# Register loads of several words in one instruction, and a softmax ahead of the edge list's wait

## The chip, the cores and the metric
The kernel runs on one core of a Trainium2 chip. Its time is that of the device for one execution, in microseconds (us); less is better. The core's engines are TensorE (PE, its weight loads PEld), VectorE (DVE), ScalarE (ACT), GpSimd (POOL) and SyncE (SP). [...] An engine's sequencer also runs small instructions of its own, such as a load of a register from memory; in the profile those stand under the engine's name with a q behind it (DVEq, PEldq).

## What is computed
A graph network on 6250 nodes with 128 features and 100000 edges sorted by their target, in four blocks. Each block ends in a layer norm of its input plus its result.

```python
x = layernorm(x + attention_by_edge_type(x))   # block 0
x = layernorm(x + three_gat_layers(x))         # block 1: 3 layers of graph attention
x = layernorm(x + edge_mlp(x, edge_attr))      # block 2
x = layernorm(x + degree_scaled_sum(x))        # block 3
# block 0
pk    = softmax(confounder_probs)              # 5 values
alpha = einsum('ehk,k->eh', leaky_relu(scores), pk)
a     = exp(alpha - segment_max(alpha)[seg]);  alpha_n = a / segment_sum(a)[seg]
out   = segment_sum(xj * alpha_n * importance[type], dst) + x @ W[0] + bias
# a layer of block 1
e     = leaky_relu(alpha_s[src] + alpha_d[dst])
alpha = exp(e - segment_max(e)[dst]) / (segment_sum(...)[dst] + 1e-16)
out   = segment_sum(xs[src] * alpha, dst) + bias
# block 2
h = relu(concat(x[src], edge_attr) @ w1a + b1a); h = relu(h @ w1b + b1b); h = h @ w1c + b1c
agg = segment_sum(h, dst) / max(count, 1);  z = relu(concat(x, agg) @ w2a + b2a) @ w2b + b2b
# block 3
agg = segment_sum((deg**-0.5 * x)[dst], src);  out = relu(deg**-0.5 * agg @ weight.T)
```

## The kernel before
The start counts degrees with matmuls of one-hot rows (`STEPS` turns of two halves: DVE compares at L490 and L492, PE counts at L733), orders the nodes by degree and lays out records: with each group of edges, which rows of a node table to gather, and the number of the tile of target nodes that the sum is added to. In its first microseconds SP issues the DMA of the edge list and 14 weight DMAs in a row; POOL lays constants and then fills a large tile with zeros (L433); DVE splits the edge list into high and low parts (L469 to L473), waits for all weights and makes the softmax of the five mixture probabilities (L476 to L484), with ACT's exponential (L800) in its middle; PE multiplies the weights with the attention vectors (L742 to L746) and then counts.

Every later block is a loop in which POOL issues indirect DMAs. Each fetches 128 rows of a table by their numbers, or in the last block adds 128 rows to a table. The order of the work is written out by hand: each engine has its own loop over items, and semaphores free buffers.

- Layer 0 (gathers L986): items of three groups, two buffers. ACT lays out the slots (`lay_slots`, L1009, whose places in `win` it loads at L1012), makes exponentials, and keeps the running sums in `acc` at a tile number (`keep`, loads at L1047 and L1048).
- Graph attention (`gat`, L1588; gathers L1716, 16 per batch, 50 batches a layer). DVE makes the scores (`scores`), then for each half of the heads (`f` = 0, 1) the products of weights and gathered rows (L1859 to L1863) and a running sum along the slots (the scan L1872). After the second half's products it frees the batch's gather buffer (`used`), after the scans it copies the last column of each group to its tile in `acc1` (L1881). It needs two tile numbers (L1877) and two columns (L1875), each read into a register with a `value_load`. While it does so, ACT copies and writes the hidden edge features of the next block (L1797), which PE multiplies (L1727).
- Edge MLP (gathers L2012 and L2017, five per item, 224 items). DVE adds the two gathered parts (`join`, L2087), PE transposes (L2038) and multiplies (L2048), ACT applies the first ReLU (L2069), DVE adds the second ReLU to `total` at the item's tile (L2109), whose number it reads at L2104. SP fetches these numbers four items at a time (`fetch_tiles`) when DVE has freed the buffer (`tiles_free`, L2114).
- Scatter (L2449, four per item, 200 items). PE makes the messages of an item with a matrix of `same` target and `h` at four tile numbers (L2257), which it reads at L2254; ACT copies them out of PSUM (L2319), POOL adds them to memory.

A `value_load` is three sequencer instructions: the load of one word (TENSOR_LOAD), arithmetic on it (FUSED_REGOPS) and a check of its bounds (SEQ_ASSERT).

## Time and profile before
| what | us |
|---|---|
| median of 3 runs | 9856.31 (9853.96 to 9918.93) |
| the profiled execution: its own time | 9892.94 |
| its span | 9891.2 |
| TensorE, busy | 4460.2 (45%) |
| VectorE, busy | 5073.3 (51%) |
| ScalarE, busy | 1673.0 (17%) |
| GpSimd, busy | 5779.6 (58%) |

The mean granted clock of TensorE was 0.666 of its full speed. Busy time counts the engines' own operations; the sequencers' loads and waits are not in it. The start takes the first 443 us, layer 0 goes to 2110, the graph attention layers to 3550, 4920 and 6282, the edge MLP from 6375 to 8215, the scatter from 8270 to 9780; between them stand short stages without gathers. In the rows below "[5.40 <-DMA soft]" behind an operation is the time its engine sat idle before it and what released it; "issue" is idle time in which nothing that the profile shows was waited for, and "remote" a semaphore whose sender the profile doesn't name.

### The profile page before, as it was taken

The page shows a single profiled execution, that of the slowest core. Times are in us where ns is not written, and L with a number is a line of the kernel's source. Part 1 is how long each engine was busy: PE and PEld are TensorE (multiplying, and loading weights), DVE is VectorE, ACT ScalarE, POOL GpSimd, SP SyncE. Part 2 cuts the span into 40 slices and gives each one's busy share as a digit, 9 for nine tenths or more (in the row PEclk, how much of TensorE's full clock was granted, in tenths as well). Part 3 has the DMA queues.
Part 4 walks back from the last instruction along what each step waited for, and adds up shares of the span by engine and source line. Part 5 has one row for each costly group of instructions (what it writes and reads, how often), then busy time and mean ns, then how long its engine had stood idle before and what let it go on. Part 6 is the DMA issues. An engine that isn't in the chain of part 4 may idle for free. (4 is left out here: it accounts for less than half of the span.)

```text
span 9891.2 us, 83332 instructions
## 1 busy us (share of the span) xinstructions
PE 4460.2 (45%) x14438; PEld 2760.1 (28%) x14438; DVE 5073.3 (51%) x11750; ACT 1673.0 (17%) x3458; POOL 5779.6 (58%) x5435
## 2 busy tenths in 40 slices
PE   6266676762333332222232222366666666554442
PEld 5122232232222222212121121233333333343332
DVE  7266676674555544544544444444444444554443
ACT  1322222231111111111111111211111111110002
POOL 2455555525655545555555555455556555888886
PEclk8688888875555565555565555677778777765555
DMA  2422222234332323333233333344444444444444
GB/s 59 134 51 51 52 53 54 53 40 132 90 87 79 85 69 83 87 83 89 78 89 84 88 84 83 97 127 126 133 131 134 127 125 51 36 36 36 36 36 85
DMA packets 673823, 804.66 MB, mean 81 GB/s; under 512 B 312241, under 2 KB 513273, under 8 KB 672600
## 3 DMA queue, kind: packets, MB, share of 16 engines
q0 software_dynamic: 317520, 531.92, 26.6%
q1 hardware_dynamic: 313896, 114.11, 4.5%
q10 hardware_dynamic: 42336, 157.90, 4.5%
q14 instruction: 51, 0.42, 0.0%
q8 instruction: 20, 0.33, 0.0%
HBM read 578.06 MB, written 225.40 MB: 81 GB/s over the span
## 5 line engine op out<-in xcount | busy, mean ns | idle before, releaser
L1716 POOL DMA_INDIRECT big<-table_layer,slot_rows_L x2400 | 2298.3, 958 | 1726.5 <-issue 1138.5
L2449 POOL DMA_INDIRECT sums_by_source<-big,to x800 | 1261.3, 1577 | 282.2 <-issue 202.8
L986 POOL DMA_INDIRECT big<-table_layer,idx_L x912 | 931.7, 1022 | 767.0 <-DVE h L1160 442.1
L1735 PE MATMUL own_ps_L<-of_tile_L,big 50*128 50x16 f32 x1224 | 283.1, 369 | 2327.1 <-DVE fade_L L1850 1406.0
L2017 POOL DMA_INDIRECT big<-table_layer,rec_m x904 | 866.8, 959 | 275.4 <-issue 270.5
L2109 DVE SCALAR_TENSOR_TENSOR big<-ps,nbb,big 128x128 f32 x1792 | 545.8, 346 | 923.6 <-remote 592.6
L2048 PE MATMUL ps<-big,w 128*128 128x512 f32 x1792 | 914.3, 658 | 135.5 <-ACT big L2069 103.8
L1735 PEld LDWEIGHTS own_ps_L<-of_tile_L,big 50*128 50x128 f32 x1224 | 271.3, 324 | 2406.0 <-issue 2397.6
L1727 PE MATMUL psH_L<-w,h 128*128 128x256 f32 x1584 | 676.3, 606 | 462.2 <-ACT big L1797 385.1
L1078 PE MATMUL sums_L<-h,ident 128*128 128x512 f32 x1344 | 706.1, 674 | 322.1 <-issue 165.4
L1872 DVE TENSOR_TENSOR_SCAN big<-h,products_L 128x1122 f32<-128x1122 f32 x300 | 747.5, 2492 | 25.4 <-issue 1.0
L2257 PE MATMUL psM<-h,big 128*128 x1600 | 383.9, 415 | 618.5 <-issue 618.5
L1727 PEld LDWEIGHTS psH_L<-w,h 128*128 128x128 f32 x1584 | 484.9, 317 | 589.4 <-issue 282.1
L1797 ACT ACTIVATE big<-psH_L 128x1536 f32<-128x1536 f32 (+1 forms) x144 | 193.6, 1344 | 2657.8 <-DMA h<-in_edges 1545.0
L1863 DVE TENSOR_TENSOR products_L<-products_L,big 128x512 f32<-128x512 f32 x600 | 612.2, 1066 | 0.0
L1859 DVE COPY products_L<-big 128x66 f32<-128x66 f32 x300 | 82.5, 275 | 929.9 <-ACT products_L L1785 524.2
L2038 PE MATMUL psX<-ident,big 128*128 128x128 f32 x1800 | 299.5, 321 | 558.9 <-DVE big L2087 500.8
L2069 ACT ACTIVATE big<-psX,ba 128x512 f32<-128x512 f32 x450 | 283.5, 684 | 1573.2 <-remote 991.7
L2012 POOL DMA_INDIRECT big<-hidden_edge_parts,rec_m x226 | 213.0, 942 | 543.5 <-DVE big L2087 426.6
L2257 PEld LDWEIGHTS psM<-h,big 128*128 128x128 f32 x1600 | 330.6, 305 | 684.3 <-issue 684.3
L2048 PEld LDWEIGHTS ps<-big,w 128*128 128x128 f32 x1792 | 369.3, 218 | 529.1 <-issue 430.4
L1078 PEld LDWEIGHTS sums_L<-h,ident 128*128 128x128 f32 x1344 | 281.8, 217 | 754.2 <-issue 737.4
(445 smaller groups left out, 7361.0 us busy)
## 6 DMA issues: line engine op xcount, KB each, us to landing
hidden_edge_parts<-big ACTq DMA_DIRECT2D x72, 768.0 KB
hidden_edge_parts<-big ACTq DMA_DIRECT2D x72, 640.0 KB
big<-table_layer,slot_rows_L POOLq DMA_INDIRECT x2400
h<-in_edges ACTq DMA_DIRECT2D x75, 384.0 KB
h<-in_edges ACTq DMA_DIRECT2D x75, 320.0 KB
table_layer<-xr SPq DMA_DIRECT2D x49, 298.0 KB
big<-table_layer,idx_L POOLq DMA_INDIRECT x912
big<-table_layer,rec_m POOLq DMA_INDIRECT x904
```

Of the source, the lines that this page charges most:

```text
L986: G.indirect_dma_start(out=g[b][:, u, s, :], out_offset=None, in_=table, in_offset=bass.IndirectOffsetOnAxis(ap=at, axis=0)).then_inc(gath ...
L1078: PE.matmul(sums[b][u][:, 0:T * D], ident[:, :], prod[PROD[u]][:, s, :], start=(s == 0), stop=False, skip_group_check=True)
L1716: G.indirect_dma_start(out=ring[b][:, s, :], out_offset=None, in_=tab1_d[l], in_offset=bass.IndirectOffsetOnAxis(ap=at_rows[b][:, s, R_POS ...
L1727: last = PE.matmul(psH[:, c * HID:(c + 1) * HID], eT[b % 2][:, c * P:(c + 1) * P], w1[:, 1, :], start=True, stop=True)
L1735: last = PE.matmul(own_ps[:, c * SLOTS:(c + 1) * SLOTS], own1T[:, c * P:(c + 1) * P], of_tile[b % 2][:, :], start=True, stop=True)
L1863: last = V.tensor_tensor(p4[:, c, 0:C, 1:SLOTS + 1], bc(wt[:, hd, :], 1, C), ring[b][:, :, hd * C:(hd + 1) * C].rearrange("p s c -> p c s" ...
L1872: V.tensor_tensor_scan(flat(tot[b % 2][:, rows, :]), flat(shrink[:, rows, :]), flat(prod[:, :, :]), 0.0, ALU.mult, ALU.add)
L2017: G.indirect_dma_start(out=gx[u][:, s, :], out_offset=None, in_=tab2_d, in_offset=bass.IndirectOffsetOnAxis(ap=rec[q][:, a, s * FW + R_POS ...
L2048: last = PE.matmul(ps2[u % 2][:, f * S * P:(f + 1) * S * P], w2[:, k, f * P:(f + 1) * P], h1[u % 2][:, k * S * P:(k + 1) * S * P], start=( ...
L2109: V.scalar_tensor_tensor(t, ps2[u % 2][:, (f * S + s) * P:(f * S + s + 1) * P], nbb[:, f:f + 1], t, ALU.max, ALU.add)
L2257: last = PE.matmul(psM[v][:, s * P:(s + 1) * P], same[v][:, s, :], flat(h[:, ds(js[s], 1), :]), start=True, stop=True)
L2449: G.indirect_dma_start(out=sum_d[s], out_offset=bass.IndirectOffsetOnAxis(ap=to[u][:, s:s + 1], axis=0), in_=msg[u][:, s, :], in_offset=No ...
```

## The change
Two things. First, in all gather loops one `load` reads several neighbouring words of a tile into several registers, and a `snap` for each register gives the value with its bounds; before, each value had a `value_load`. In the graph attention the tile numbers are copied beside the columns into one tile of four words (`places`), with one more cast in `scores`, and all four are read in the second half, behind its scan. In the edge MLP the four tile numbers of four items are read at the first of them, and the buffer is freed right behind that load. Second, the probabilities are SP's first DMA, with a semaphore of their own, and DVE makes their softmax before it waits for the edge list; the other waits for weights count 13 instead of 14 DMAs.

```diff
--- before.py
+++ after.py
@@ -276,6 +276,7 @@
             edges_in = sem("edges_in_d")
             cst2 = sem("consts_first")
             w_in = sem("weights_in")
+            probs_in = sem("probs_in")
             x_in = sem("features_in")
             wp = sem("score_weights_done")
             w_ok = sem("score_weights_copied")
@@ -329,14 +330,14 @@
 
             @block.sync
             def _(sp):
+                sp.dma_start(soft[:, :], probs.partition_broadcast(P)).then_inc(probs_in, 16)
                 sp.dma_start(e32[:, :], dst).then_inc(edges_in, 16)
                 for to, frm in ((wT[:, :, :], W0T), (aI[:, :], attI), (aJ[:, :], attJ),
                                 (rhs0[:, :, 0:D], W0), (bias[:, 0, :], bias0.partition_broadcast(P)),
                                 (wsT[:, :, :], WsT), (wdT[:, :, :], WdT),
                                 (aS[:, :, :], attS), (aD[:, :, :], attD), (rhs1[:, :, 0:D], Ws),
                                 (impt[:, :], importance.partition_broadcast(P)),
-                                (bias[:, 1:4, :], bias1.partition_broadcast(P)), (bias1T[:, :], bias1cols),
-                                (soft[:, :], probs.partition_broadcast(P))):
+                                (bias[:, 1:4, :], bias1.partition_broadcast(P)), (bias1T[:, :], bias1cols)):
                     sp.dma_start(to, frm).then_inc(w_in, 16)
                 sp.dma_start(xTs[:, :], xT).then_inc(x_in, 16)
                 sp.sem_inc(rec_out, 64)
@@ -432,7 +433,7 @@
 
                 G.memset(pool1[:, :], 0.0).then_inc(blank, 1)
                 pool.wait_ge(cst2, NCONST)
-                pool.wait_ge(w_in, 16 * 14)
+                pool.wait_ge(w_in, 16 * 13)
                 G.tensor_tensor(out=rhsN[:, 0:D], in0=rhs0[:, 0, 0:D], in1=ident[:, :], op=ALU.add)
                 pool.wait_ge(w_ok, 1)
                 pool.wait_ge(soft_ok, 1)
@@ -465,6 +466,16 @@
                 for v in range(STG):
                     last = V.memset(stage[v][:, :, A0:A0P], 0.0)
                 last.then_inc(pos_blank, 1)
+                dve.wait_ge(probs_in, 16)
+                V.tensor_reduce(tot[:, 0:1], soft[:, :], AX.X, ALU.max)
+                dve.drain()
+                V.tensor_scalar(soft[:, :], soft[:, :], tot[:, 0:1], None, ALU.subtract).then_inc(mx, 1)
+                dve.wait_ge(ex, 1)
+                V.tensor_reduce(tot[:, 1:2], soft[:, :], AX.X, ALU.add)
+                dve.drain()
+                V.reciprocal(tot[:, 2:3], tot[:, 1:2])
+                dve.drain()
+                V.tensor_scalar(soft[:, :], soft[:, :], tot[:, 2:3], None, ALU.mult).then_inc(soft_ok, 1)
                 dve.wait_ge(edges_in, 16)
                 V.tensor_scalar(part[0][:, :], e32[:, :], P - 1, None, ALU.bitwise_and)
                 V.tensor_scalar(part[1][:, :], e32[:, :], 7, None, ALU.arith_shift_right)
@@ -472,16 +483,6 @@
                 V.tensor_copy(lo[:, :], part[0][:, :])
                 V.tensor_copy(hi[:, :], part[1][:, :])
                 dve.drain()
-                dve.wait_ge(w_in, 16 * 14)
-                V.tensor_reduce(tot[:, 0:1], soft[:, :], AX.X, ALU.max)
-                dve.drain()
-                V.tensor_scalar(soft[:, :], soft[:, :], tot[:, 0:1], None, ALU.subtract).then_inc(mx, 1)
-                dve.wait_ge(ex, 1)
-                V.tensor_reduce(tot[:, 1:2], soft[:, :], AX.X, ALU.add)
-                dve.drain()
-                V.reciprocal(tot[:, 2:3], tot[:, 1:2])
-                dve.drain()
-                V.tensor_scalar(soft[:, :], soft[:, :], tot[:, 2:3], None, ALU.mult).then_inc(soft_ok, 1)
                 dve.wait_ge(cst2, NCONST)
                 with dve.Fori(0, STEPS) as i:
                     for v in range(2):
@@ -737,7 +738,7 @@
                     pe.sem_inc(c, 1)
                 pe.wait_ge(cst2, NCONST)
                 PE.matmul(histp[:, 0:NT], zerob[:, :], zerob[:, 0:NT], start=True, stop=False)
-                pe.wait_ge(w_in, 16 * 14)
+                pe.wait_ge(w_in, 16 * 13)
                 for t in range(T4):
                     PE.matmul(wps[:, t * 40:t * 40 + 20], wT[:, t, :], aJ[:, :], start=True, stop=True)
                     PE.matmul(wps[:, t * 40 + 20:t * 40 + 40], wT[:, t, :], aI[:, :], start=True, stop=True)
@@ -1009,7 +1010,8 @@
                     def lay_slots(b, i):
                         act.wait_ge(slots_out[b], i * 32 + 32)
                         act.sem_inc(gate_a, 1)
-                        at = [0] + [act.value_load(spot[b][0:1, u:u + 1], min_val=0, max_val=SLOTS - S) for u in range(1, B)]
+                        act.load(spot_r, spot[b][0:1, 1:B])
+                        at = [0] + [act.snap(r, min_val=0, max_val=SLOTS - S) for r in spot_r]
                         A.activation(flat(win[b][:, :, :]).bitcast(u16), flat(padw[:, :, :]).bitcast(u16), ACT.Copy)
                         A.drain()
                         for u in range(B):
@@ -1031,6 +1033,8 @@
                     act.sem_inc(tiles_read, 2)
                     act.sem_inc(shr_ok, 1)
                     n = turns(act)
+                    tile_r = [act.alloc_register(f"tile_{tag}_r{u}") for u in range(B - 1)]
+                    spot_r = [act.alloc_register(f"spot_{tag}_r{u}") for u in range(1, B)]
                     exps(0, 0, 0)
                     shrinks(0, 0)
                     lay_slots(0, 0)
@@ -1045,7 +1049,8 @@
                         for b in range(2):
                             k = i * 2 + b
                             js = [act.value_load(tile[1 - b][0:1, B - 1:B], min_val=0, max_val=NT)]
-                            js += [act.value_load(tile[b][0:1, u:u + 1], min_val=0, max_val=NT) for u in range(B - 1)]
+                            act.load(tile_r, tile[b][0:1, 0:B - 1])
+                            js += [act.snap(r, min_val=0, max_val=NT) for r in tile_r]
                             A.drain().then_inc(tiles_read, 1)
 
                             act.wait_ge(z_ok, k + 1)
@@ -1597,7 +1602,7 @@
                     of_tile = [sb(f"of_tile_{tag}{v}", [NTP, SLOTS], fp32, ph) for v in range(2)]
                     same = sb(f"same_tile_{tag}", [1, GPB, GS], fp32, ph)
                     in_tile = sb(f"slots_in_tile_{tag}", [1, GPB], fp32, ph)
-                    last_col = sb(f"last_column_{tag}", [1, GPB], i32, ph)
+                    places = sb(f"tile_and_column_{tag}", [1, 2 * GPB], i32, ph)
                     z = sb(f"z_{tag}", [P, H, SLOTS], fp32, ph)
                     zc = sb(f"zc_{tag}", [P, H, SLOTS + 1], fp32, ph)
                     lift = sb(f"lift_{tag}", [P, H, SLOTS + 1], fp32, ph)
@@ -1838,7 +1843,8 @@
                             V.tensor_reduce(in_tile[:, :], same[:, :, :], AX.X, ALU.add)
                             V.scalar_tensor_tensor(z[:, :, :], z[:, :, :], 0.2, z[:, :, :], ALU.mult, ALU.max)
                             dve.drain()
-                            V.tensor_copy(last_col[:, :], in_tile[:, :])
+                            V.tensor_copy(places[:, GPB:2 * GPB], in_tile[:, :])
+                            V.tensor_copy(places[:, 0:GPB], tiles[:, :, 0])
                             V.tensor_scalar(zc[:, :, 1:SLOTS + 1], z[:, :, :], LOW, None, ALU.max)
                             dve.drain()
                             V.tensor_tensor_scan(flat(run_max[:, :, :]), flat(lift[:, :, :]), flat(zc[:, :, :]), 0.0,
@@ -1872,10 +1878,9 @@
                                 V.tensor_tensor_scan(flat(tot[b % 2][:, rows, :]), flat(shrink[:, rows, :]), flat(prod[:, :, :]),
                                                      0.0, ALU.mult, ALU.add)
                                 if f:
-                                    ks = [dve.value_load(last_col[0:1, u:u + 1], min_val=1, max_val=GS) for u in range(GPB)]
-                                else:
-                                    js = [dve.value_load(fl[b][0:1, GS * u, R_J:R_J + 1], min_val=0, max_val=NT)
-                                          for u in range(GPB)]
+                                    dve.load(places_r, places[0:1, :])
+                                    js = [dve.snap(r, min_val=0, max_val=NT) for r in places_r[0:GPB]]
+                                    ks = [dve.snap(r, min_val=1, max_val=GS) for r in places_r[GPB:]]
                                 dve.drain()
                             for u in range(GPB):
                                 V.tensor_copy(flat(acc1[:, ds(js[u], 1), :]),
@@ -1933,6 +1938,7 @@
                             V.tensor_tensor(brow[:, :], brow[:, :], psB[0:4, :], ALU.add).then_inc(rows_read, 1)
                         dve.drain()
                         n = turns_of_batches(dve)
+                        places_r = [dve.alloc_register(f"tile_or_column_{tag}{u}") for u in range(2 * GPB)]
                         one_hot(0, 0)
                         both_loops(dve, n, turn)
                         if counting:
@@ -2092,6 +2098,7 @@
                     dve.sem_inc(summed, 2)
                     dve.sem_inc(joined, U)
                     n = turns(dve)
+                    tile_r = [dve.alloc_register(f"tile_m_r{a}") for a in range(Q)]
                     join(0, 0)
                     join(0, 1)
                     with dve.Fori(0, n) as i:
@@ -2100,8 +2107,11 @@
                             join(*following(*following(i, u)))
                             if u % Q == 0:
                                 dve.wait_ge(tiles_in[q], i * 16 + 16)
-                            dve.sem_inc(gate_v, 1)
-                            j = dve.value_load(tiles[q][:, u % Q, R_J:R_J + 1], min_val=0, max_val=NT)
+                                dve.sem_inc(gate_v, 1)
+                                dve.load(tile_r, tiles[q][:, :, R_J])
+                                js = [dve.snap(r, min_val=0, max_val=NT) for r in tile_r]
+                                dve.sem_inc(tiles_free[q], 1)
+                            j = js[u % Q]
                             dve.wait_ge(lin2, g + 3)
                             for s in range(S):
                                 for f in range(2):
@@ -2110,8 +2120,6 @@
                                                            ALU.max, ALU.add)
                                 last = V.drain()
                             last.then_inc(summed, 1)
-                            if u % Q == Q - 1:
-                                dve.sem_inc(tiles_free[q], 1)
 
             fresh_semaphores()
             added = [sem(f"added_{s}") for s in range(S)]
@@ -2251,7 +2259,8 @@
                         pe.wait_ge(same_ok, g + 1)
                         pe.wait_ge(msg_ok, g + 1)
                         pe.sem_inc(gate_pe, 1)
-                        js = [pe.value_load(rec[u][0:1, s, R_J:R_J + 1], min_val=0, max_val=NT) for s in range(S)]
+                        pe.load(tile_r, rec[u][0:1, :, R_J])
+                        js = [pe.snap(r, min_val=0, max_val=NT) for r in tile_r]
                         pe.sem_inc(tiles_read, 1)
                         for s in range(S):
                             last = PE.matmul(psM[v][:, s * P:(s + 1) * P], same[v][:, s, :], flat(h[:, ds(js[s], 1), :]),
@@ -2271,6 +2280,7 @@
                             if early and u == 5:
                                 output(q, n)
 
+                    tile_r = [pe.alloc_register(f"tile_s_r{s}") for s in range(S)]
                     pe.sem_inc(msg_ps, 2)
                     pe.sem_inc(tiles_read, U)
                     for w in range(2):
```

## Rows read from the trace of the kernel before

**Rows 1.** Windows by stage: us, busy us (count) of PE, PEld, DVE, ACT, POOL; clock, DMA, GB/s.
```profile
443.00:2110.00 1667.00, 1129.08 (x2212) 457.21 (x2213) 1116.77 (x2460) 362.17 (x1053) 931.70 (x912) 0.83 0.31 52
...
3620.00:4920.00 1300.00, 319.44 (x931) 253.03 (x930) 608.97 (x1236) 168.04 (x146) 755.61 (x800) 0.55 0.31 85
...
6375.00:8215.00 1840.00, 1153.90 (x3559) 603.48 (x3560) 852.85 (x2655) 280.44 (x446) 1079.79 (x1130) 0.79 0.47 130
8270.00:9780.00 1510.00, 682.06 (x2788) 539.40 (x2788) 675.16 (x1778) 171.54 (x332) 1261.29 (x800) 0.59 0.41 36
```
**Rows 2.** Waits in the scatter, 8350 to 9700: us in total, times, longest.
```profile
POOL sums_by_source L2449 <- issue: 181.1, 594, 0.3
```
**Rows 3.** Waits in the edge MLP, 6500 to 8050.
```profile
DVE big L2109 <- remote: 488.3, 62, 12.0
...
POOL big L2012 <- DVE big L2087: 361.9, 65, 9.2
```
**Rows 4.** Timeline in the edge MLP: start us, us, operation, count [idle before <-releaser].
```profile
7206.21 3.60 PE L2048 MATMUL ps<-big,w 128*128 128x512 f32 x8
...
7212.85 0.95 POOL L2017 DMA_INDIRECT big<-table_layer,rec_m  x1 [0.30 <-issue]
7215.30 2.66 DVE L2109 SCALAR_TENSOR_TENSOR big<-ps,nbb,big 128x128 f32 x8 [10.07 <-remote]
...
7218.08 1.43 DVE L2087 TENSOR_TENSOR big<-big 128x256 f32<-128x256 f32 x4
...
7220.34 0.94 POOL L2012 DMA_INDIRECT big<-hidden_edge_parts,rec_m  x1 [6.54 <-DVE big L2087]
```
**Rows 5.** Timeline of the start, DVE.
```profile
3.90 2.06 DVE L469 TENSOR_SCALAR pool<-pool 128x784 int32<-128x784 int32 x1 [2.84 <-DMA pool<-in_dst]
...
7.15 0.64 DVE L473 CAST hi_d<-pool 128x784 bf16<-128x784 int32 x1
...
13.42 13.40 DVE L478 TENSOR_SCALAR soft<-soft,tot 128x5 f32<-128x5 f32 x1
...
27.93 1.09 DVE L490 TENSOR_TENSOR oneL<-lo_d,wide 128x1792 bf16<-128x1792 bf16 x1
```
**Rows 6.** Timeline of the start, POOL.
```profile
10.50 15.87 POOL L433 MEMSET pool<- 128x18944 f32 x1
```
**Rows 7.** Lines, 0 to 443: count, busy us, mean ns, idle before and releasers.
```profile
L490 DVE TENSOR_TENSOR oneL<-lo_d,wide 128x1792 bf16<-128x1792 bf16 x56 | 61.2, 1093 | 7.9 <-PE histp L733 7.8
```
**Rows 8.** Timeline of the start, PE.
```profile
18.77 0.57 PE L746 MATMUL wps<-aD,wdT 128*128 128x4 f32 x2
29.54 0.67 PE L733 MATMUL histp<-oneH,oneL 128*128 128x49 bf16 x5 [10.19 <-DVE oneH L492]
```
**Rows 9.** Instructions of line 1877: count, ns min/median/max, first and last start.
```profile
L1877 DVEq TENSOR_LOAD <-slot_records_L x300: 7/302/1029, 2265.2 to 6291.9; - x150
L1877 DVEq FUSED_REGOPS  x300: 190/190/728, 2266.1 to 6292.2; - x150
```
**Rows 10.** Timeline in the second graph attention layer.
```profile
4218.65 2.49 DVE L1872 TENSOR_TENSOR_SCAN big<-h,products_L 128x1122 f32<-128x1122 f32 x1
...
4221.21 0.27 DVE L1859 COPY products_L<-big 128x66 f32<-128x66 f32 x1
...
4224.27 0.94 POOL L1716 DMA_INDIRECT big<-table_layer,slot_rows_L  x1 [16.77 <-issue]
```
**Rows 11.** Waits in the second graph attention layer, 3800 to 4600.
```profile
DVE big L1881 <- issue: 72.6, 62, 7.1
```
**Rows 12.** Instructions of line 1012 in layer 0.
```profile
L1012 ACTq TENSOR_LOAD <-spot_L x171: 272/277/283, 470.1 to 2125.2; - x171
```
**Rows 13.** Waits in layer 0, 600 to 2100.
```profile
ACT big L1024 <- DVE carry_L L1173: 119.0, 38, 7.1
```
**Rows 14.** Instructions of line 2254 in the scatter.
```profile
L2254 PEldq TENSOR_LOAD <-rec_s x800: 293/298/397, 8267.9 to 9718.0; - x160
```

## What I predict

> **What bounds the kernel now.** I read the busy times by stage first, then what GpSimd's gathers wait for in each stage, then single stretches in order of time. The page's average (POOL 58% busy) says little, since the stages differ [rows 1]. In the last stage, the scatter, POOL is busy 1261.29 of 1510 us in 800 DMA issues of 1.58 us, and its idle time there is "issue" of 0.3 us between two of them [rows 1, 2]: it never waits for another engine's result, so whatever TensorE's loads cost there is off the path. In the gather stages POOL issues in bursts and then stands: 1667 - 931.70 = 735 us idle in layer 0, 1300 - 755.61 = 544 us in a graph-attention layer, 1840 - 1079.79 = 760 us in the edge MLP [rows 1]. Part of it is the 0.3 us behind each of 800 to 1130 gathers. The rest are true pauses: in the edge MLP POOL waited 361.9 us for the join of DVE, and DVE's sums waited 488.3 us for "remote" [rows 3].
>
> One pause in order of time shows the chain [rows 4]. TensorE began its matmuls at 7206.21, but DVE's sums of their result start at 7215.30, 1.5 us after POOL's last gather of the burst (7212.85 + 0.95). The sums take 2.66 us, the join behind them 1.43, and POOL restarts at 7220.34. No register load is exposed in that chain: sums end at 7217.96, the join starts at 7218.08. So this pause is one of completions that come late, not of address arithmetic. The question for every load that the change drops is whether it lies in such a chain or under another instruction.
>
> **The softmax ahead of the edge list.** Now DVE splits the edge list (3.90 on), waits for the last of the weight DMAs, and then its subtraction of 128x5 stands from 13.42 for 13.40 us, to 26.82; the one-hot loop starts at 27.93 [rows 5]. POOL has been filling a 128x18944 tile from 10.50 to 26.37 [rows 6], so the subtraction stood behind the fill. TensorE had finished its weight products at 19.34 (18.77 + 0.57) and counts from 29.54 [rows 8].
> After the change the probabilities are the first DMA and should land by about the 3.90 at which the first one now does. The bitwise operation issued at 3.90 ended at 5.96 [rows 5], beside POOL's first constant, so I let the subtraction end there too; from the subtraction's end to the loop the exponential, sum, reciprocal and product took 27.93 - 26.82 = 1.1 us [rows 5]: softmax done at 7.1. The four edge operations take 4 x 0.64 = 2.6 us [rows 5] and end at 9.7. The fill starts at 10.50. The loop can start at about 10.6, 17 us earlier; but TensorE is in order behind its weight products, whose DMAs are unchanged but for one, so it counts from 19.34 instead of 29.54: **-10.2 us**. The loop itself is DVE's (56 x 1.09 us for the larger half alone, and 7.8 us waiting for TensorE) [rows 7], and the ordering, scores and table follow its end, so I count the shift in full.
> It hangs on the loop's first comparison running beside the fill. No row shows a two-input DVE operation beside a POOL fill; the only operation beside it, the subtraction, was held to its end. By the pessimist's end the comparison starts at 26.4 and the shift is 29.54 - 28.2 = **-1.3**; the optimist's end, were TensorE not in order, is -17. I take -10, as the comparison is another kind of operation.
> [...]
>
> **Graph attention, three layers.** Each of 150 batches reads two tile numbers after DVE's first scan and two columns after the second; the change reads all four after the second, and casts two more values. One value costs a load of 0.30 us and 0.19 for its register arithmetic [rows 9], with check and gaps about 0.6; two are 1.2 us, issued when the scan starts. The scan takes 2.49 us (4218.65 to 4221.14) and the next operation starts at 4221.21 [rows 10]: both pairs lie wholly under a scan. Four words in one load are 0.30 + 4 x 0.28 = 1.4 us, also under it. The cast adds some 0.2 us per batch, 30 us in all of DVE, but the stage waits on POOL. So nothing in most batches.
> There are stretches in which a sequencer instruction takes 0.7 us (maxima 1029 for the load, 728 for the arithmetic) [rows 9]; the accumulating copies behind them sat idle up to 7.1 us, 72.6 us in 62 times [rows 11]. There two values cost 6 x 0.7 = 4.2 us, 1.7 us beyond the scan. The first pair is ahead of the products that free the ring for POOL, so its removal takes 1.7 us off; the second block grows to 9 x 0.7 = 6.3 us, 3.8 beyond its scan, but POOL had restarted by then (4224.27, during the second scan [rows 10]). An estimate: a quarter of 100 batches in two layers x 1.7 = 43 us of DVE, of which a quarter is in the chain that POOL waits for (72.6 us of such idle against 544 of pauses says no more): **-10 us**, between -75 (each slow batch counts, both blocks) and +15 (the cast in half the batches).
>
> **Edge MLP.** DVE read one tile number per item; now it reads four at every fourth, 56 times. One took 0.30 us [rows 9] and was issued under the 1.43 us join [rows 4]: hidden, so the three dropped gain nothing. Four words are issued just behind the join's four operations and end 1.4 us later, an estimated 0.3 us after it; in about half the items DVE waits on a late completion anyway [rows 3]. 56 x 0.3 x 1/2 = **+8 us**, between 0 and +59 (56 x 1.05, each further word 0.2 us more). Freeing the tile buffer before the sums instead of after the fourth lets SP fetch sooner, four items ahead: nothing waits for that DMA now.
> [...] No multi-word load is in this trace; the single one took 0.30. [...]
>
> **Layer 0.** ACT reads three slots in one load instead of three, 57 times, and three tiles in one (0.28 us for a load [rows 12]): at most 2 x 57 x 2 x 0.28 = 64 us of ACT's sequencer. Those are ahead of a wait for DVE's carry (119.0 us in 38 waits [rows 13]), so what ACT gains it waits. POOL's pauses here end with DVE's own work, which no changed instruction feeds directly: **-3**, between -20 and 0.
>
> **Scatter.** TensorE drops 3 of 4 loads per item, 200 x 3 x 0.30 = 180 us [rows 14] of its own idle time. POOL's 7.5 us per item covers it [rows 1, 2]: **0**.
>
> **The sum.** -10 -10 -3 +8 = -15 us. Against the profiled run's own 9892.94 that is 9878; that run lies 36.6 us above the median, so on the median 9856.31 it gives **9841**.
>
> **Rivals.**
> A. *The fill blocks the comparison, or the edge operations are late.* If the last cast is issued after 10.50, or the comparison collides, the start gives 1.3 instead of 10. For: the held subtraction, and only 0.8 us of room. Against: another kind of operation. 9850. Chance 0.25.
> B. *Bursts join (faster).* A pause costs about 7 us (7213.80 to 7220.34 [rows 4]). If DVE's shorter sequencer work lets a batch's buffer come free before POOL runs dry, whole pauses vanish: 5 in each attention layer are 105 us, 9841 - 105 = 9736. For: pauses, not gathers, are what can shrink; slow stretches hold DVE up. Against: the chain behind a pause shows no load. 0.14.
> C. *Bursts split (slower).* In the attention layers DVE's block after the second scan is longer. POOL restarts during that scan and has two buffers of 16 gathers, 2 x 20 us; if the block delays the next freed buffer by over about 5 us, each such batch costs a pause of 7 us; with the edge MLP's +59 in place of +8, and four pauses in each layer, 9841 + 51 + 84 = 9976. It decides at 5 us; by my count the slow block is 2.1 us longer than before (3.8 - 1.7). 0.06.
> D. *One instruction is not one cost:* the load is split or pays by word, so the loads give nothing and only the start remains: 9846 to 9871. 0.15.
>
> **The numbers.** 1% is what a measurement of this kernel can tell, 98.6 us: 9757.7 and 9954.9. The forecast itself has 0.40; with A and D that is 0.80 within 1%, from about 9790 to 9890. B gives 0.14 faster, C 0.06 slower. For 8 in 10 the range leaves out most of B and of C: the low end is -75 in the attention layers (9841 - 65 = 9776), the high end the +59 of the edge MLP, or D, or a few split bursts (9841 + 51 = 9892): 9775 to 9890.
>
> **What would show it.** The subtraction at about 4 to 6 us; the first comparison at 10.6 (or 26.4: A); TensorE's first count at about 19.4. In the attention layers the scan followed by the next copy within 0.1 us, as now, and idle before the accumulating copies no longer than before. In the edge MLP an "issue" idle of 0.2 to 0.4 us at every fourth item (1 us: D). In the scatter less idle of TensorE and the same stage time. Wrong would be: a stage of gathers that moves by over 40 us either way while its POOL busy time stays, since then pauses, not loads, changed.

## The result and the profile after

The changed kernel took 9786.39 us (median of 4 runs, 9761.33 to 9800.99), the kernel before 9870.99 in the runs beside it: ratio 0.990 (95% interval 0.9866 to 0.9934), 85 us less. The profiled execution took 9785.20 us, 107.7 less than that of before. I had forecast 15 us.

First the windows by stage, as in [rows 1] (us, busy us and count of PE, PEld, DVE, ACT, POOL; clock, DMA share, GB/s), each cut around the stage's gathers:

```profile
431.00:2067.00 1636.00, 1124.60 (x2213) 456.42 (x2214) 1115.11 (x2459) 361.40 (x1055) 944.16 (x912) 0.83 0.31 54
2190.00:3514.00 1324.00, 408.15 (x1745) 327.02 (x1745) 706.64 (x1379) 198.65 (x170) 785.17 (x801) 0.55 0.34 93
3588.00:4855.00 1267.00, 315.71 (x928) 251.80 (x928) 613.28 (x1279) 168.04 (x146) 756.98 (x800) 0.56 0.32 87
4912.00:6180.00 1268.00, 322.62 (x946) 254.48 (x946) 622.07 (x1290) 168.04 (x146) 759.90 (x800) 0.56 0.32 88
6272.00:8109.00 1837.00, 1169.50 (x3560) 596.33 (x3560) 855.94 (x2656) 279.24 (x444) 1082.30 (x1130) 0.79 0.47 130
8165.00:9671.00 1506.00, 693.05 (x2776) 541.08 (x2776) 669.23 (x1774) 171.00 (x331) 1261.20 (x800) 0.57 0.41 36
```

POOL's busy time in the second attention layer is what it was (756.98 against 755.61), so the stage is shorter by pauses alone. From the first to the last gather the stages changed so: layer 0 -31 us, attention layers +8, -32 and -33, edge MLP 0, scatter 0; the first gather starts 12 us earlier. The idle times of POOL over 1 us, called its pauses from here on, went from 32 to 24 and from 32 to 25 in attention layers 2 and 3.

The start, DVE, then POOL's fill, then PE (against [rows 5, 6, 8]):

```profile
4.14 1.43 DVE L472 TENSOR_SCALAR soft<-soft,tot 128x5 f32<-128x5 f32 x1
...
8.18 0.66 DVE L484 CAST hi_d<-pool 128x784 bf16<-128x784 int32 x1
10.47 1.09 DVE L491 TENSOR_TENSOR oneL<-lo_d,wide 128x1792 bf16<-128x1792 bf16 x1 [1.64 <-POOL rgrid L431]
...
19.22 1.09 DVE L491 TENSOR_TENSOR oneL<-lo_d,wide 128x1792 bf16<-128x1792 bf16 x1 [5.80 <-PE histp L734]
```
```profile
10.07 15.91 POOL L434 MEMSET pool<- 128x18944 f32 x1
```
```profile
17.15 0.57 PE L747 MATMUL wps<-aD,wdT 128*128 128x4 f32 x2
17.58 2.79 PE L734 MATMUL histp<-oneH,oneL 128*128 128x49 bf16 x28
```

The subtraction takes 1.43 us instead of 13.40, and the comparison runs its usual 1.09 us inside the fill. TensorE counts from 17.58 instead of 29.54; DVE waits 5.80 us for its first count.

In the kernel before each `value_load` of L1877 left three records on DVE's sequencer, 300 TENSOR_LOADs and 300 FUSED_REGOPS [rows 9] and as many checks (count, ns min/median/max):

```profile
L1877 DVEq SEQ_ASSERT  x300: 5/23/730, 2266.4 to 6292.4; - x150
```

The loads after, in the order graph attention, layer 0, edge MLP, scatter:

```profile
L1881 DVEq TENSOR_LOAD <-tile_and_column_L x150: 338/351/1228, 2228.1 to 6192.2; - x150
L1013 ACTq TENSOR_LOAD <-spot_L x57: 694/701/712, 458.8 to 2081.7; - x57
L2111 DVEq TENSOR_LOAD <-tiles_m x56: 947/954/976, 6293.2 to 8100.9; - x56
L2262 PEldq TENSOR_LOAD <-rec_s x200: 987/994/1107, 8160.1 to 9606.4; - x100
```

On DVE four neighbouring words took 0.35 us, on DVE and TensorE four that lie a record apart 0.95 and 0.99, on ACT three neighbours 0.70. No FUSED_REGOPS or SEQ_ASSERT stands at those lines any more: the words are used as loaded, one FUSED_REGOPS follows at the next line (medians of 0.08 us at L1014, 0.10 at L2263, 0.12 at L1882 and L2112), and the page counts 78407 instructions instead of 83332.

And the idle time of DVE before its accumulating copies in the second attention layer (3750 to 4850), before and then after:

```profile
DVE big L1881 <- issue: 109.5, 82, 7.1
```
```profile
DVE big L1886 <- issue: 18.0, 88, 0.2
```

That is the second thing to see: 1.3 us per copy became 0.2, and the longest idle fell from 7.1 us to 0.2. The slow stretches are not gone, though. Among the operations of `scores` the same kind of idle is as long as before or longer (one operation of them in the same window, before and then after):

```profile
DVE run_max_L L1844 <- issue: 20.2, 20, 1.2
```
```profile
DVE run_max_L L1850 <- issue: 48.8, 14, 3.9
```

Counted from first to last gather of attention layers 2 and 3, DVE's "issue" idle in `scores` was 210 and 217 us and is 222 and 209; where nothing pauses (after_c, below) it is 1 us at most. SyncE still has 139 and 143 small instructions of 0.7 us (148 and 163 before; 685 to 735 ns, drains left out). What is gone is DVE's long idle behind its two scans.

### The profile page after: what moved, and what is told of

It reads as the page before. It is cut to its first block and busy times, and to the rows that moved or that the text cites. A ratio compares the mean times of both kernels' runs of the same rounds, so it can differ in the third digit from the quotient of the medians.

```text
span 9783.2 us, 78407 instructions
## 1 busy us (share of the span) xinstructions
PE 4485.3 (46%) x14438; PEld 2759.3 (28%) x14438; DVE 5075.9 (52%) x11900; ACT 1671.1 (17%) x3458; POOL 5792.4 (59%) x5435
```

## The experiments

Theory S: where POOL gathers in long bursts, sequencer instructions of DVE, ACT and SP are at times served one per 0.70 us; the change helps because DVE and ACT issue far fewer register instructions (DVE 2 a batch in place of 12). Rival M: it helps because one read stands in place of several. Rival P: it helps because no load stands ahead of the products that free the ring.

**The setting.** One fact cuts through all runs. On four chips (numbers 3, 11, 15 and 2) the kernel before took 8208 to 8210 us, on four others (8, 7, 1 and 0) 9824 to 9906, like the first measurement. The program is the same and POOL's busy time nearly so; POOL's pauses over 1 us add up to 37, 34, 15, 15 and 0 us in the five gather stages (soft_only, chip 3) instead of 466, 296, 305, 305 and 435. Below, a chip "pauses" or it doesn't; there is one trace for each variant, and those of the pausing kernels come from several chips. From first to last gather, in us (the first row is the trace of before; "one-word", "padded" and "moved" are the variants described below):

| trace | pauses | first gather at | layer 0 | att. 1 | att. 2 | att. 3 | MLP | scatter |
|---|---|---|---|---|---|---|---|---|
| before | yes | 443 | 1665 | 1312 | 1295 | 1299 | 1835 | 1505 |
| after | yes | 432 | 1634 | 1321 | 1263 | 1266 | 1835 | 1505 |
| after_again | yes | 431 | 1617 | 1313 | 1270 | 1252 | 1855 | 1504 |
| l0_only_b | yes | 439 | 1618 | 1305 | 1297 | 1279 | 1825 | 1507 |
| gat_single_b (one-word) | yes | 442 | 1628 | 1325 | 1260 | 1270 | 1821 | 1505 |
| gat_padded_c (padded) | yes | 435 | 1650 | 1331 | 1288 | 1279 | 1811 | 1509 |
| gat_moved_c (moved) | yes | 444 | 1675 | 1368 | 1297 | 1296 | 1831 | 1508 |
| mlp_tail_b | yes | 433 | 1660 | 1288 | 1299 | 1272 | 1841 | 1506 |
| soft_only | no | 401 | 1257 | 1046 | 1012 | 1016 | 1425 | 1504 |
| gat_only | no | 410 | 1255 | 1048 | 1012 | 1016 | 1425 | 1507 |
| after_c | no | 399 | 1254 | 1051 | 1013 | 1016 | 1428 | 1502 |

**1. The parts alone, where nothing pauses** (chip 3). Each is the kernel before with one part of the diff shown ahead.

> The kernel before with the softmax move alone. In the trace of the changed kernel the first gather of layer 0 started 11.6 us earlier (431.5 against 443.1). Theory: the whole of that is the softmax move, since the DVE comparison runs beside POOL's fill and TensorE's first count moves from 29.54 to 17.58; ratio 0.9988 (-12 us), first gather at 431 to 432, and every later stage as long as before: layer 0 1665, attention layers 1312, 1295 and 1299, edge MLP 1835, scatter 1505 us, each within 10 us. Rival: an earlier start shifts how GpSimd's bursts fall against the other engines and so part of the 31 us of layer 0 or of the 32 and 33 us of attention layers 2 and 3 shows here too; then one of those stages is over 15 us shorter.

Ratio 0.9988 (0.9979 to 0.9998), first gather at 401 where the others have 408 to 412: the whole gain of the start, as expected.

> The kernel before with the graph attention's part alone (four words in one load behind the second scan). Theory: DVE's stretches of 0.7 us per sequencer instruction disappear with two thirds of the register instructions; the 33.2 and 31.8 us that DVE lost between first scan and next product in layers 2 and 3 come back in full, so those two layers take about 1263 and 1266 us instead of 1295 and 1299, the first layer 1312 to 1320, total -57 us, ratio 0.9942. Rival 1: the gain of those layers came from elsewhere (start, layer 0, chance of a run), and they stay within 10 us of before. Rival 2, what the prediction had: -10 us.

> The kernel before with layer 0's part alone (two loads of three words on ACT). Theory: layer 0 takes about 1634 us instead of 1665 (-31), by fewer sequencer instructions of ACT in the chain behind the exponentials; all else as before, ratio 0.9969. Rival 1: ACT's loads are ahead of a wait anyway (the prediction): within 5 us of 1665. Rival 2: the 31 us were a run's chance or came with the earlier start.

> The kernel before with the edge MLP's and the scatter's parts alone. Theory: neither is on the path of POOL; edge MLP 1835 and scatter 1505 us as before within 8 us, ratio 1.000. The four-word loads take 0.95 (DVE) and 0.99 us (TensorE) each, against 0.30 for one word. Rival: each loses its own way, the edge MLP by 56 x 0.65 = 36 us of DVE for the longer load, so a ratio of 1.004.

1.0003 (0.9993 to 1.0012), 1.0004 (0.9994 to 1.0013) and 0.9995 (0.9985 to 1.0004). Every load is hidden here, as the prediction had it, and so neither gain of theory S appears; these expectations had been made for a kernel with pauses.

**2. The whole change again** (chip 8, which pauses).

> The changed kernel once more, against the kernel before. In the runs of the four parts the kernel before took 8208 us, not 9856, and GpSimd's pauses in the gather stages were 37, 34, 15, 15 and 0 us instead of 466, 296, 305, 305 and 435; the parts other than the softmax moved nothing. Theory: where those pauses are missing, only the start is left of the change: -10 us, ratio 0.9988, with the five gather stages as long as in the kernel before within 5 us. Where they are there (before at about 9860), the ratio is 0.990 again, with layer 0 and attention layers 2 and 3 some 31, 32 and 33 us shorter. Rival: the parts work only together, and the ratio is 0.99 in either setting.

9770.59 against 9906.13 us, ratio 0.9865 (0.9816 to 0.9914): the gain is real where POOL pauses; whether it is more than in the first measurement the two intervals don't tell.

**3. What in the attention part helps.** gat_single keeps four one-word loads in their old places and takes the values as loaded:

```diff
-  ks = [dve.value_load(last_col[0:1, u:u + 1], min_val=1, max_val=GS) for u in range(GPB)]
+  for u in range(GPB):
+      dve.load(places_r[GPB + u], last_col[0:1, u:u + 1])
+  ks = [dve.snap(r, min_val=1, max_val=GS) for r in places_r[GPB:]]
...
+  (the same for js, behind the first scan)
```

gat_padded takes the changed attention part and adds dummy reads behind its scans:

```diff
+  for _ in range(1 if f else 2):
+      dve.value_load(places[0:1, 0:1], min_val=0, max_val=NT)
```

gat_moved is the kernel before with the branch of `js` put under `if f:` beside `ks`, each still a `value_load`.

Their first runs, and gat_only twice more, fell on chips without pauses:

> The graph attention's part alone once more; what matters is whether the kernel before has its pauses in this run (about 9860 to 9910 us) or not (about 8208). Theory S: DVE's sequencer instructions inside long gather bursts are served one per 0.70 us; fewer of them means that DVE no longer meets this, so attention layers 2 and 3 take about 1265 us each instead of 1295, the first one as before, ratio 0.994, and the idle between first scan and next product is 0.07 us in every batch. Rival: those layers gain only with the other parts, ratio 1.000. Without pauses: 1.000 under both.

> The four-word load as in the change, and beside it two dummy one-word reads with their checks in the first half's place and one in the second's, so that DVE's queue again has as many register instructions as before; the values used come from the one load. Theory S (the number of instructions): the 0.7 us stretches return and most of the gain goes, ratio 0.998 to 1.000, with 25 to 35 us of excess idle behind the first scan in layers 2 and 3. Rival M (one read of memory instead of four dependent ones behind the copies): the gain stays, ratio 0.994. Without pauses: 1.000.

> The kernel before with its four one-word loads at their old places, but each value taken straight from its register, so without the arithmetic and bounds check behind each load: 4 sequencer instructions a batch instead of 12, no load of several words, no extra cast. Theory S: nearly the whole gain, ratio 0.994 to 0.996, so the load of several words is not what helps. Rival M: no gain, 1.000. Without pauses: 1.000.

> The kernel before with the two tile numbers read behind the second scan, beside the columns, four one-word loads with their checks: as many instructions as before, but none ahead of the products that free the ring. Theory P (place): the 33 us per layer that lay behind the first scan are what POOL waited for, so layers 2 and 3 gain about 30 us each though the slow stretches stay behind the second scan, ratio 0.994. Theory S alone: stretches move with the instructions, the block behind the second scan grows by 30 us a layer and POOL gains part of it at most, ratio 0.996 to 1.000. Without pauses: 1.000.

> The graph attention's part alone, again in the hope of a chip on which the kernel before pauses (two of three so far had none: 8208 us; one had them: 9906 us). With pauses, theory S (fewer sequencer instructions of DVE): attention layers 2 and 3 about 30 us shorter each, no idle over 0.1 us between first scan and next product, ratio 0.994; layer 0, edge MLP and scatter as in the kernel before. Rival: the gain needs the other parts. Without pauses: 1.000.

1.0002, 1.0002, 0.9996 and 1.0002 (chip 11), 1.000 (chip 15), every interval within 0.0015 of 1. They tell nothing of the theories. Then chip 7, which pauses:

> Four one-word loads at their old places without arithmetic and checks behind them, again for a setting with pauses. With pauses, theory S (the number of sequencer instructions): attention layers 2 and 3 gain 25 to 33 us each, ratio 0.994 to 0.996, and the idle behind the first scan is gone. Rival M (the one load of four words): 1.000. Without pauses: 1.000.

Ratio 0.9978 (0.9959 to 0.9996), attention layers 2 and 3 at 1260 and 1270 us. With no load of several words, the long idle behind the scans is gone (3750 to 4850):

```profile
DVE big L1884 <- issue: 18.4, 86, 0.5
```

Six register instructions a batch are left of twelve, and DVE still has 41 and 46 small instructions of 0.7 us in layers 2 and 3 (195 and 198 before). Rival M as the only cause is out. The ratio is smaller than I expected, though the two layers came out as expected; the runs of before on this chip have a low median (9824.4).

> Layer 0's part alone, again for a setting in which the kernel before pauses. With pauses: layer 0 takes 1615 to 1635 us against 1665, the later stages as in the kernel before, ratio 0.996 (fewer instructions of ACT's sequencer inside gather bursts). Rival: 1.000, the gain of layer 0 needs the earlier start. Without pauses: 1.000.

Layer 0 took 1618 us, but the ratio is 0.9990 (0.9972 to 1.0009): a gain in the trace that the times don't make certain.

On chip 2 nothing pauses:

> The one four-word load plus three dummy one-word reads with their checks, so DVE has its old number of sequencer instructions; again for a setting with pauses. Theory S (number): the excess idle behind DVE's first scan is back (25 to 35 us in each of layers 2 and 3), these layers take 1290 to 1300 us, ratio 0.998 to 1.001. Rival M (one read in place of several is what helps): 1260 to 1270 us each, no excess idle, 0.994 to 0.997. Without pauses: 1.000.

> All four values read one by one with their checks, behind the second scan; again for a setting with pauses. Theory P (only what stands ahead of the ring-freeing products counts): no idle behind the first scan, layers 2 and 3 at 1260 to 1270 us though the stretches behind the second scan stay, ratio 0.996. Theory S with the block's length counting in full: the excess of 33 us moves behind the second scan (from 67 to about 100 us) and the layers stay at 1280 to 1300 us, ratio 0.998 to 1.001. Without pauses: 1.000.

> The changed kernel on the same chip as the two before it. With pauses: ratio 0.988 to 0.993, start 10 us, layer 0 10 to 45 us, attention layers 2 and 3 together 55 to 75 us shorter than in the kernel before. Without pauses, theory: only the start is left, ratio 0.9988; rival: the parts add up to more, under 0.997.

1.0005 (0.9996 to 1.0015), 1.0003 (0.9993 to 1.0012) and, for the whole change, **0.9986 (0.9976 to 0.9995)**: only the start is left. Then chip 1, which pauses:

> As gat_padded_b. With pauses, theory S (number of sequencer instructions): excess idle of 25 to 35 us behind DVE's first scan in each of attention layers 2 and 3, 1290 to 1300 us each. Rival M (one read in place of several): 1260 to 1270 us each and no excess idle. Without pauses: 1.000.

Ratio 1.0031 (1.0004 to 1.0057), layers 2 and 3 at 1288 and 1279. The same line, then the dummy reads' arithmetic here and in the run of the same kernel on a chip without pauses:

```profile
DVE big L1883 <- issue: 83.5, 84, 5.6
```
```profile
L1880 DVEq FUSED_REGOPS  x450: 5/197/710, 2244.7 to 6284.3; - x150
```
```profile
L1880 DVEq FUSED_REGOPS  x450: 190/197/203, 1823.3 to 5022.4; - x150
```

With nearly the old number of instructions (11) the long idle is back, although one load reads all four words: theory S. The excess behind the first scan is smaller than expected (23.6 and 10.1 us, not 25 to 35), and the two layers lie at the low end of the kernels with that idle. The attention part of the change by itself fell on chips without pauses all three times; where POOL pauses it was seen only within the whole change. The last two rows show that the 0.7 us belongs to the setting, not to the instruction: the longest of 450 is 203 ns there.

> As gat_moved_b. With pauses, theory P (only what stands ahead of the ring-freeing products counts): no idle behind the first scan, attention layers 2 and 3 at 1260 to 1270 us, ratio 0.996. Theory S with the block's length counting in full: the layers stay at 1280 to 1300 us, ratio 0.998 to 1.002. Without pauses: 1.000.

```profile
DVE big L1880 <- issue: 194.4, 84, 14.2
```

Ratio 1.0066 (1.0028 to 1.0103) on chip 0: slower than before. No idle is left behind the first scan, yet layers 2 and 3 stay at 1297 and 1296, while the idle behind the second grew from 109.5 to 194.4 us. Rival P is out: emptying one place and filling the other gives nothing. The kernel is slower, as rival C had it for a longer block behind the second scan, but not by its mechanism: POOL has no more pauses than before (30, 31 and 32 in the three layers against 31, 32 and 32), and most of the loss is in layer 1, 1368 us against 1312, where they add up to 354 us against 296.

> The edge MLP's and the scatter's parts alone, for a setting with pauses. Theory: the four-word load of 0.95 us stands behind every fourth join and delays sums and the next burst, edge MLP 1840 to 1855 us, ratio 1.001 to 1.003; the scatter 1505 us as before. Rival: hidden by the late completions, edge MLP 1810 to 1835 us, ratio 1.000. Without pauses: 1.000.

Ratio 1.0002 (0.9974 to 1.0030), edge MLP 1841 us, scatter 1506. Waits of the sums for completions (DVE L2109 and its like, 6500 to 8050) are no fewer than in [rows 3]:

```profile
DVE big L2113 <- remote: 562.6, 77, 14.2
```

The three traces with this part have 1835 to 1855 us (mean 1844), the five without it 1811 to 1835 (1825). A cost of up to 19 us fits, the times neither confirm nor exclude it.

## Why the prediction was wrong, step by step

**What bounds the kernel.** Right in that no load stood in the chain of [rows 4], and that pauses are what can shrink. But I took the pauses for the kernel's own. Where they are missing, the edge MLP of the changed kernel waits so (5280 to 6600 of after_c):

```profile
DVE big L2093 <- DMA big<-table_layer,rec_m: 384.8, 172, 5.3
...
DVE big L2119 <- PE ps L2054: 67.6, 37, 3.5
...
POOL big L2018 <- issue: 59.7, 196, 0.3
```

No wait of DVE's sums for "remote" is left (488.3 us in [rows 3]), and POOL's gathers of this stage are never kept longer than 0.3 us. The program is the same but for the change; the late completions of [rows 4] don't show here.

**The start.** Right: forecast -10, measured 12 us in the trace and 0.9988 alone (on the pausing chips the first gather comes at 431 and 432 us with the part, at 433 to 444 without it). The comparison ran beside the fill: 1.09 us inside one of 15.91. That it would, being another kind of operation than the held subtraction, was my assumption; no row of before showed it, and no run shows why the subtraction was held and the comparison not. The comparison at 25.72, beside POOL's addition at 25.95 that reads two tiles, took 1.64. TensorE's products ended at 17.72, 1.6 us sooner than in [rows 8], which is the rest of the 12 us. Rival A did not happen; the last cast was issued at 8.18, 1.9 us ahead of the fill.

**Graph attention: the step that failed.** I put -10 us: 25 slow batches of 1.7 us are 43 us of DVE, a quarter of that on the path, and the block behind the second scan counted nothing, as POOL had restarted by then. What was mis-sized is the 43 us. In the trace of before the idle between first scan and next product exceeds 0.6 us in 7 and 8 of 50 batches of layers 2 and 3, with 33.2 and 31.8 us in all: 4 to 5 us a batch. Behind the second scan and between the copies there are another 97 and 101 us more than after the change. All of DVE's "issue" idle fell from 459 and 466 us to 332 and 332, by 261 us, and the two layers by 65: a quarter. In gat_single_b the idle fell by 368 us and the layers by 64, a sixth. So in these kernels the share was about right, and the idle six times what I had. The share is no constant: in gat_moved_c the idle is 137 us more than before and the two layers are as long.

I had it too small for three reasons that the traces show. The drains and address operations around the register instructions are served at the same pace, and I had not counted them: of DVE's 367 and 380 sequencer instructions of 685 to 735 ns in layers 2 and 3 of before, 172 and 182 are drains, and 23 and 26 the address operations of L1881. At times DVE gets only one in 1.4 us, with one of SyncE between (below). And I gave the new block nine instructions, one load and an arithmetic and a check for each word, where it has two. That the block behind the second scan is not free gat_moved_c shows.

That the stretches stay, as the sum assumed, was right: DVE still meets them in `scores`, and now also just ahead of the scans (33 and 27 us of "issue" idle against 1 and 0). But in none of the 100 batches does it stand over 0.1 us behind the first scan or over 0.5 us behind the second and between the copies.

Traces without long idle behind the scans (after, after_again, gat_single_b) have 2522 to 2530 us for layers 2 and 3 together, the five with it 2567 to 2594: -53 us on average. Part of it is given back in layer 1: 1313 to 1325 us against 1288 to 1312 in the three traces with the old attention part (gat_padded_c and gat_moved_c have 1331 and 1368). No run shows a cause. Over all three layers it is 3835 to 3855 against 3859 to 3906, 35 us on average.

**Layer 0.** I put -3, on the argument that ACT's time ahead of a wait is lost anyway. Three traces with the part have 1617 to 1634 us (mean 1623), five without it 1628 to 1675 (1656). But gat_single_b, without the part, has 1628, and the times of the part alone give -10 with an interval from -28 to +9. So the -31 of the first trace lies outside my bound of -20, and how much of it the part makes stays open.

**Edge MLP and scatter.** +8 and 0 forecast; 0 to +19 and 0 measured. The load of four took 0.95 us, where one word took 0.30 (L2104 of before): (0.954 - 0.303) / 3 = 0.217 us for each further word. No row of the kernel before shows the 0.2 us for a further word behind my +59 of the range; in its place the runs showed this 0.217, on TensorE (0.994 - 0.298) / 3 = 0.232, and on ACT, for neighbours, (0.701 - 0.277) / 2 = 0.212. In the attention layers four neighbours took 0.351 on DVE, where one had taken 0.311 (L1875 of before). Rival D was so far right: in three of the four places the load took about 0.2 us longer for each further word. In after_c the "issue" idle before the sums is never over 0.3 us, as forecast.

**The rivals.** What came nearest is B, fewer and longer bursts, at 0.14; I priced it at 105 us by 15 lost pauses, and 15 were lost (8 and 7) for 70 us. The three traces without the long idle have 24 or 25 pauses in each of these layers, the other five 26 to 32. I argued against it that the pause in [rows 4] showed no load. That pause was in the edge MLP, where nothing was gained; the case had to be read in the attention layers, whose [rows 11] showed the 7.1 us.

**The sum.** By the averages above, where POOL pauses: start -8 to -12, layer 0 up to -33, layer 1 +18, layers 2 and 3 -53, MLP up to +19: about -60 of the 85 and 135 us measured. The rest lies between the stages and in the spread of a kernel that pauses (before: 9854 to 9954 us on chip 8 alone). How these share out is not settled. That 9786 lies inside my range is owed to its low end, the -75 of the attention layers, not to the -10.

What serves the sequencers once per 0.70 us, and why only some chips do it, no run shows. That it is one thing shared by DVE and SyncE is suggested by the records at 4011 us of the trace of before, where DVE and SyncE take turns: SP at 4011.56, DVE 4012.27, SP 4012.96, DVE 4013.67.

## What to carry to other kernels

Before costing a load by its own duration, look at its minimum, median and maximum: a maximum that small instructions of different kinds share can mean that their number is the price. Here it was 728 and 730 ns for the arithmetic and the check at L1877 of before, whose medians are 190 and 23: in the slow stretches they cost as much as each other. Drop small instructions first: with six a batch in place of twelve the long idle behind the scans was gone (gat_single_b, attention layers 2 and 3 at 1260 and 1270 us). What merging loads gives has to be measured for each engine and layout: on DVE four neighbours took 0.35 us and four words a record apart 0.95, on ACT three neighbours 0.70. And when a stage is full of waits that nothing explains, measure on more than one chip before reading them as the kernel's structure: here they were worth some 1650 us, and most of what the change won: without them it won 12.

## What was not expected of the hardware

- The same program takes 8208 us on some chips and 9824 to 9906 on others, with POOL's busy time, in the traces of this kernel and its variants, at 5757 to 5766 us on the first and 5773 to 5811 on the others.
- A register load of four words takes 0.35 us for neighbours on DVE and 0.95 to 0.99 for words a record apart (DVE, TensorE); three neighbours on ACT took 0.70.
- A 128x1792 comparison of two SBUF operands ran at its usual 1.09 us beside POOL's fill, a 128x5 subtraction of a scalar operand had taken 13.40 us beside it and ended at 26.82, 0.45 us behind the fill's end.
